# Pre-norm attention and top-2 mixture-of-experts layer on one Trainium2 core: the projected values are copied out of PSUM by ScalarE, and their bias is folded into the output projection's bias

## What is computed

```python
def _L0_attn_ref(x, W_attn, b_attn, W_proj, b_proj):
    qkv = x @ W_attn + b_attn
    q, k, v = jnp.split(qkv, 3, axis=2)
    ...
    q = _rope_as_in_source(q)
    k = _rope_as_in_source(k)
    att = jnp.einsum('bhqd,bhkd->bhqk', q, k) * (1.0 / math.sqrt(hd))
    att = jnp.where(causal[None, None, :, :], att, -jnp.inf)
    att = jax.nn.softmax(att, axis=-1)
    y = jnp.einsum('bhqk,bhkd->bhqd', att, v)
    y = y.transpose(0, 2, 1, 3).reshape(B, T, C)
    return y @ W_proj + b_proj

x = x + _L0_attn_ref(_layernorm(x, axis=-1), ...)
x = x + _L0_ffn_ref(_layernorm(x, axis=-1), ...)
```

## Time and profile before

| | |
|---|---|
| median of 3 runs | 1797.29 us (1796.71 to 1798.85) |
| the profiled execution, its own time | 1802.63 us |
| its span, first to last instruction | 1800.9 us |
| mean granted TensorE clock | 0.976 of full speed |
| instructions | 45470 |
| attention, loop of 16 batches | about 55 to 860 us of the span |

### The profile page before, as it was taken

One profiled execution on the slowest core, in us unless ns is written; L12 is line 12 of the kernel. 1 busy time (PEld: TensorE's weight loads), 2 busy tenths in 40 slices (PEclk: granted clock), 3 DMA queues, 4 the chain that ended last, 5 costly groups with the idle time before them and its releaser, 6 DMA issues.

```text
span 1800.9 us, 45470 instructions
## 1 busy us (share of the span) xinstructions
PE 1636.0 (91%) x15505; PEld 1132.7 (63%) x15507; DVE 1169.6 (65%) x2062; ACT 874.3 (49%) x1273; POOL 780.0 (43%) x1005
## 2 busy tenths in 40 slices
PE   2689999999999999984798999989999999999996
PEld 2345555555555555432575566669999999999985
DVE  5568888888888888874358777874434444443442
ACT  1266666666666666552333222544444444444442
POOL 1023333333333333332200676725666666666652
PEclk9799999999999999987899999999999999999998
DMA  1322333333333333211536553223434333333432
GB/s 58 106 84 83 107 106 107 106 99 101 104 106 107 107 99 96 91 54 43 187 124 185 171 164 88 83 89 54 68 59 66 62 62 66 61 64 61 65 60 25
DMA packets 168709, 163.37 MB, mean 91 GB/s; under 512 B 29682, under 2 KB 159218, under 8 KB 168563
## 3 DMA queue, kind: packets, MB, share of 16 engines
q1 hardware_dynamic: 138354, 125.66, 22.8%
q0 software_dynamic: 30208, 35.81, 12.4%
HBM read 100.82 MB, written 60.30 MB: 89 GB/s over the span
## 4 chain that ended last, share of the span: by engine, by line
PE 68%; DVE 12%; issue 7%; DMA 5%; SPq 4%; ACT 3%; POOL 1%; DVEq 0%; POOLq 0%; ACTq 0%
PE bank L1615 21%; PE pair_s L1980 10%; PE pair_s L1615 7%; PE bank L1980 5%; PE pair_t L1980 5%; PE bank L1749 4%; PE pair_s L1675 3%; SPq L480 2%; PE pair_t L1723 2%; DVE mx L1165 2%; PE pair_t L1969 2%; ACT qkh L861 2%; SPq L472 1%; DMA q_op<-m_row 1%; PE bank L1765 1%
## 5 line engine op out<-in xcount | busy, mean ns | idle before, releaser
L884 ACT ACTIVATE prob<-pair_t 128x1024 f32<-128x1024 f32 x320 | 327.4, 1023 | 243.0 <-PE pair_t L1723 238.3
L702 POOL TENSOR_SCALAR_AFFINE_SELECT prob<-prob 128x256 f32<-128x256 f32 (+1 forms) x448 | 196.8, 453 | 478.0 <-ACT prob L884 466.4
L818 POOL DMA_INDIRECT out_x<-ysb,tok_rows x136 | 218.2, 1605 | 196.2 <-ACT ysb L1025 146.3
L1573 DVE SCALAR_TENSOR_TENSOR early<-pair_s,h_s,sg 128x512 f32<-128x512 f32 (+1 forms) x72 | 51.9, 721 | 249.0 <-PE pair_s L1980 249.0
L780 POOL DMA_INDIRECT tok_d<-tok_w,dest_i x128 | 126.6, 989 | 160.2 <-DVE dest_i L1424 121.5
L1980 PE MATMUL pair_s<-xt,wbuf 128*128 128x256 f16 (+1 forms) x1728 | 193.9, 267 | 1.9 <-DVE xt L1564 1.9
L1615 PE MATMUL bank<-wbuf,early 128*128 x1632 | 190.2, 273 | 0.9 <-ACT ysb L1025 0.8
L1749 PE MATMUL bank<-prob,v_op 128*32 128x512 f32 (+3 forms) x2048 | 181.5, 450 | 2.0 <-POOL prob L702 1.7
L1016 ACT CAST early<-early 128x512 f16<-128x512 f32 (+1 forms) x144 | 85.6, 594 | 196.6 <-DVE early L1573 196.6
L1615 PE MATMUL pair_s<-wsh,xt 128*128 128x512 f16 x768 | 179.2, 382 | 0.0
L1980 PEld LDWEIGHTS pair_s<-xt,wbuf 128*128 x1728 | 163.0, 98 | 22.3 <-issue 2.3
(11 more groups left out here) (259 smaller groups left out, 3090.8 us busy)
## 6 DMA issues: line engine op xcount, KB each, us to landing
q_op<-qk_d SPq DMA_DIRECT2D x192, 64.0 KB, 2.4
k_op<-qk_d SPq DMA_DIRECT2D x192, 64.0 KB, 2.4
x_in<-in_L_attn_x SPq DMA_DIRECT2D x16, 512.0 KB, 4.2
qk_d<-qkh SPq DMA_DIRECT2D x32, 256.0 KB, 2.5
qk_d<-qkl SPq DMA_DIRECT2D x32, 256.0 KB, 2.7
xres<-in_L_attn_x SPq DMA_DIRECT2D x16, 512.0 KB, 4.7
x_d<-x SPq DMA_DIRECT2D x32, 256.0 KB, 2.2
xhl_d<-xhl SPq DMA_DIRECT2D x32, 256.0 KB, 2.5
```

The costliest lines, as they stand in the source:

```text
L702: last = nc.gpsimd.affine_select(out=v, in_=v, compare_op=ALU.is_ge, fill=0.0, base=0, pattern=[[0, v.shape[1]], [1, P]], channel_multipli ...
L818: pool.indirect_dma_start(out=out, out_offset=bass.IndirectOffsetOnAxis(ap=tok_rows[:, k, 0:1], axis=0), in_=ysb[:, k % ROWS_AHEAD], in_of ...
L884: nc.scalar.activation(prob[:, half, u].rearrange("p a n -> p (a n)"), pair_t[:].rearrange("p a n -> p (a n)"), ACT.Exp, scale=exp_by).the ...
```

## The change

ACT's new `values` copies a half of the values in one instruction of 128x512 from PSUM to `v_op`, without a bias; DVE's `values` with its two additions goes. The call keeps its slot in the table, and in ACT's body it stands last among the projection's copies, so behind `normalise` in the same step. The broadcast bias row `bvb` and its DMA go. In the prologue the bias of the values is turned into two more columns of `bcol` by two more one-element matmuls, DVE spreads each column into a 128x128 tile (`bvm`), PE multiplies these with the output weights into `ps_y`, and DVE adds the result to `bpb` once, after the shift of batch 1 and ahead of its loop; POOL's first addition of `bpb` waits for that.

```diff
-        bvb = sb_a("bvb", [P, C], F32)
-        bcol = sb_a("bcol", [P, 4], F32)
+        bcol = sb_a("bcol", [P, 6], F32)
+        bvm = sb_a("bvm", [P, 2, P], F32)
...
-            sp.dma_start(bvb[:], b_attn[2 * C:].unsqueeze(0).broadcast_to([P, C])).then_inc(S["const_in"], 16)
...
-                                        pool.wait_ge(S["const_in"], 48)
+                                        pool.wait_ge(S["bias_done"], 1)
...
+            def values(n, par, j, src=ps_q):
+
+                act.wait_ge(S["v_in"], 2 * n + j + 1)
+                if n == 0:
+                    act.wait_ge(S["v_cleared"], 1)
+                if some(4 * (n - 1)):
+                    act.wait_ge(S["pv_in"], 4 * (n - 1))
+                nc.scalar.copy(v_op[:, par, 2 * j:2 * j + 2, :, 0:HD],
+                               src[:].rearrange("p (t h d) -> p t h d", t=2, d=HD)).then_inc(S["v_done"], 1)
...
-                for i in range(4):
+                for i in range(2):
+                    qk_high(0, i, QK_BANK[i])
+                for j in range(2):
+                    values(0, 0, j, V_BANK[j])
+                for i in range(2, 4):
                     qk_high(0, i, QK_BANK[i])
...
                                 if (g, s) == QK_HIGH[i] and QK_HIGH[i] >= QK[i]:
                                     qk_high(b + 1, i)
+                            for j in range(2):
+                                if (g, s) == VALUES[j]:
+                                    values(b + 1, 1 - par, j)
...
-            def values(n, par, j, src=ps_q):
-
-                dve.wait_ge(S["v_in"], 2 * n + j + 1)
-                if some(4 * (n - 1)):
-                    dve.wait_ge(S["pv_in"], 4 * (n - 1))
-                for t in range(2):
-                    last = nc.vector.tensor_tensor(
-                        v_op[:, par, 2 * j + t, :, 0:HD],
-                        src[:, 256 * t:256 * t + 256].rearrange("p (h d) -> p h d", d=HD),
-                        bvb[:].rearrange("p (h d) -> p h d", d=HD), ALU.add)
-                last.then_inc(S["v_done"], 1)
-
...
-                nc.vector.tensor_copy(bcol[:], ps_m[:, 0:4])
+                link.link(dve, nc.vector.tensor_copy(bcol[:], ps_m[:, 0:6]))
                 link.link(dve, nc.vector.tensor_copy(wah[:], wa[:, 0:2, :]))
                 nc.vector.tensor_tensor(wal[:], wa[:, 0:2, :], wah[:].bitcast(F32),
                                         ALU.subtract).then_inc(S["scales_done"], 1)
+                for c in range(2):
+                    last = nc.vector.tensor_scalar(bvm[:, c, :], ones_f[:], bcol[:, 4 + c:5 + c], None, ALU.mult)
+                last.then_inc(S["bvm_done"], 1)
...
-                dve.wait_ge(S["const_in"], 48)
+                dve.wait_ge(S["const_in"], 32)
...
-                for j in range(2):
-                    values(0, 0, j, V_BANK[j])
...
                 input_shift(1)
+                dve.wait_ge(S["bias_in"], 1)
+                nc.vector.tensor_tensor(bpb[:], bpb[:], ps_y[:, 0:C], ALU.add).then_inc(S["bias_done"], 1)
...
-                            for j in range(2):
-                                if (g, s) == VALUES[j]:
-                                    values(b + 1, 1 - par, j)
...
-                for i in range(4):
-                    col = 256 * (i % 2) + P * (i // 2)
+                for i in range(6):
+                    col = 256 * (i % 2) + P * (i // 2) if i < 4 else 2 * C + P * (i - 4)
...
                     project_qk(0, i, QK_BANK[i])
+                pe.wait_ge(S["bvm_done"], 1)
+                pe.wait_ge(S["const_in"], 32)
+                pe.wait_ge(S["xl_done"], 2)
+                for c in range(2):
+                    last = nc.tensor.matmul(ps_y[:, 0:C], bvm[:, c, :], wp[:, c, :], start=(c == 0), stop=(c == 1))
+                last.then_inc(S["bias_in"], 1)
```

More of the change, by code:

```diff
@@ L247, in build @@
         names = ("k_filled const_in w_in x_in0 x_in1 res_in ops0 ops1 qks0 qks1 "
-                 "pool_const attn_w qk_topped biascols scales_done "
+                 "pool_const attn_w qk_topped biascols scales_done bvm_done bias_in bias_done v_cleared "
                  "xn_done shift_done xnT_in xh_done xl_done qk_in qkh_done qkl_done v_in v_done "
@@ L1097, in prologue @@
                 link.link(dve, nc.vector.memset(mx[:], 0.0))
-                link.link(dve, nc.vector.memset(v_op[:, :, :, :, HD:HD + 1].rearrange(
-                    "p a t h d -> p (a t h) d"), 1.0))
+                nc.vector.memset(v_op[:, :, :, :, HD:HD + 1].rearrange(
+                    "p a t h d -> p (a t h) d"), 1.0).then_inc(S["v_cleared"], 1)
                 stats(0, 0, 0)
```

## The result

| | median | lowest to highest | ratio to the kernel before, 95% interval |
|---|---|---|---|
| kernel before, first comparison | 1797.29 us (5 runs) | 1796.71 to 1799.71 | |
| changed kernel | 1812.33 us (5 runs) | 1812.01 to 2804.05 | 1.007 [1.0057, 1.0083] |
| changed kernel, second comparison | 1811.03 us (before: 1799.98) | 1810.63 to 1813.69 | 1.0064 [1.0047, 1.0081] |
| changed kernel, third comparison | 1813.96 us (before: 1799.93) | 1812.00 to 1817.42 | 1.0081 [1.0061, 1.0100] |

The changed kernel is slower: by 15.0, 11.1 and 14.0 us between medians, and by 12.6, 11.5 and 14.6 us by the ratios, where 14.7 were forecast (1812.0 us).

The account below looks back on a forecast made before the run. PE was taken to bound a batch, busy 47.87 of 50 us. Loop terms 15.5 + 0.1 - 2.6 and prologue +1.7 gave +14.7 us on 1797.3, so 1812.0 us; own range 1807 to 1816, whole range 1804 to 1820.

Parts of the forecast that it names:

- Half 0: Loop step (1,3): ACT's single copy ends sooner than DVE's two additions, gaining 0.17 us a batch, 2.6 us in all.
- The exponential behind it: ACT's exponential after the half 0 copy: ACT is free again at 267.57, before its start at 267.75, so no delay.
- Half 1: Loop step (2,3): copy queues behind two normalisations on ACT, stalling PE 1.11 us in 14 batches, 15.5 us.
- batch 14: Half 1 without normalisations: the copy follows `o_t` directly, ends at 279.86 and costs 0.12 us.
- nothing to absorb it: PE's other waits shift with the stall; rivals: half absorbed, 1804.3 us, chance 0.08; wholly, 1796.5 us, chance 0.05.
- DVE's relief: DVE's freed 0.68 us in (1,3) and 0.69 us in (2,3) were taken to gain zero.
- the rival: Faster by relief of DVE in front of low parts and maxima: 1788.8 us, chance 0.05.
- The prologue: Bias work before the loop: +1.5 us before PE's first projection plus 0.2 us for the `bpb` addition, +1.7 us.
- The wait for the bias columns: Prologue: two more one-element matmuls, four more records of 0.21 us, lengthen DVE's wait by 0.86 us.
- the added wait and the two fills: Prologue, ahead of L1072: 0.11 us for the wait on `bcol`, 0.54 us for two `bvm` fills.
- The addition to `bpb`: Prologue, ahead of the first maximum: between nothing and 0.34 us, taken as 0.2 us.
- the gap on POOL: Prologue, 7.25 us from DVE's variance to POOL's root: moves with the chain; otherwise the estimate is 1.5 us lower.

Follow-up runs that it names:

- the kernel with the copy at (2,2): Changed kernel with ACT's copy of half 1 one step earlier, at (2,2): 1960.62 us against 1962.19, ratio 0.9992; later 1798.85 against 1799.93, ratio 0.9993.
- the two dose experiments: Changed kernel with three or one instead of two normalisations ahead of half 1's copy: 1985.17 us, ratio 1.0120, and 1967.90 us, ratio 1.0032.

## Why the prediction was right

**Half 0, gain of 0.17 us.** Measured 0.17 in the timeline (0.40 against 0.57 us), and 0.17 to 0.27 in the shortest period of the kernel with the copy at (2,2). The exponential behind it was to be late for nothing, and started 0.04 us after PE's shifted scores.

**Half 1, stall of 1.11 us in 14 batches.** Measured 1.12. The sum of both, +0.94 us a batch, came out as +0.96 in the shortest period (+0.90 between the second profiles). In batch 14 the 0.12 us of the forecast measured 0.14. That the wait goes through PE's queue in full, with nothing to absorb it, was argued from the chains behind PE's other waits; the two dose experiments show it, at 0.47 and 0.49 us for a step of 0.50.

**DVE's relief, nothing.** Right, by the kernel in which DVE is kept busy. The rule that the rival leaned on, to use both engines for emptying PSUM (the Trainium skill, TensorEngine Tiling (Array Packing), "PSUM Bottleneck"), is neither borne out nor refuted as a rule: here it gains 0.17 us a batch where ACT is free when the product ends, and loses 1.1 us where it is queued behind other work.

**The prologue, +1.7 us.** The parts hold nearly, but about 1 us of their sum arrives at the loop. DVE and POOL of the changed kernel:

```profile
33.47 0.16 DVE L1138 COPY bcol<-bank 128x6 f32<-128x6 f32 x1 [2.81 <-PE bank L1656]
...
36.34 0.48 DVE L1143 TENSOR_SCALAR bvm<-ones_f,bcol 128x128 f32<-128x128 f32 x2
36.73 1.28 DVE L1088 TENSOR_TENSOR xl<-bank,xh 128x512 fp32r<-128x512 f32 x2
...
51.84 0.17 DVE L1077 TENSOR_SCALAR mv<-mv 128x4 f32<-128x4 f32 x1
...
60.69 0.42 DVE L1159 TENSOR_TENSOR bpb<-bpb,bank 128x256 f32<-128x256 f32 x1
61.02 1.22 DVE L1172 TENSOR_REDUCE mx<-pair_s 128x2 f32<-128x1024 f32 x1
```

```profile
13.03 0.28 POOL L642 TENSOR_SCALAR_AFFINE_SELECT ident<-ident 128x128 f32<-128x128 f32 x1 [11.36 <-issue]
...
59.52 1.05 POOL L675 TENSOR_TENSOR rstd<-mv,neghalf 128x4 f32<-128x4 f32 x1 [31.18 <-issue]
```

The wait for the bias columns is 2.81 us instead of 1.96, +0.85 (0.86 forecast). From `bcol` to L1088 it is 3.26 us instead of 2.74, +0.52 (0.65 forecast for the added wait and the two fills; the fills take 0.39 of it, start to start). The addition to `bpb` holds the first maximum up by 0.33 (0.2 forecast). That is +1.7. Yet the first maximum is at 61.02 and was at 61.35. First, the whole chain hangs on POOL's first select, and that one starts at 13.0 to 14.4 us from trace to trace; in the trace of before:

```profile
14.22 0.28 POOL L643 TENSOR_SCALAR_AFFINE_SELECT ident<-ident 128x128 f32<-128x128 f32 x1 [12.54 <-issue]
```

Counted from there, L1088 comes 1.4 us later with the bias work in every trace: 23.69 to 23.73 us in ten, against 22.32 and 22.35 in the two of the kernel before and 22.32 with the work off the path. The maximum comes after 47.99 us instead of 47.13 (second profiles: 48.86 and 47.81), so only +0.9 and +1.05 of the +1.7 are left there; over the ten traces it is 47.63 to 49.01. The rest goes in two places that vary from trace to trace. One is the gap on POOL, below. The other is the way from L1088 to the end of the variance, 15.28 us instead of 16.40 (16.20 and 16.38 in the second profiles), in which PE's first products run: their records go from 0.63 to 0.39 us each, and this happens at 41.7 us in the changed kernel's trace and at about 44 us before, while the granted clock reads 1.00 in both. Over the traces, the sooner it happens after L1088 the shorter that way is; in both traces of the kernel before it happens latest. Why is not shown.

**The gap on POOL moves with the chain.** From the variance's end to the root it is 7.25 us before and 7.51 after, 7.91 and 7.44 in the second profiles, and over the 13 traces used here it is 7.15 to 7.91 us while the variance ends anywhere from 51.56 to 53.94. So it isn't a time of its own that would swallow a delay. The Trainium skill (GPSIMD Engine Reference, "Instruction dispatch") gives about 6 us for the first call of a freshly loaded routine, without an instruction of its own in the profile. A gap of that kind is what the traces have, somewhat longer; that a load fills it no run shows.

**The total.** 14 times 0.96, and about 1 us from the prologue, is 14.4 us; measured 15.0, 11.1 and 14.0 between medians. The ratios' intervals are 10.2 to 14.9, 8.5 to 14.6 and 11.0 to 18.0 us: the first and the third hold the forecast difference of 14.7, the second just ends below it. That the forecast is on the high side fits two readings above: the prologue gives 1 us instead of 1.7, and averaged over all twelve periods the batch grows by 0.75 to 0.98 us instead of 1.11 less 0.17. Whether a tenth of a us of each stall is given back in the longer batches isn't settled.

## What to carry to other kernels

If the engine that bounds the stage waits for a piece of work, moving that work from a nearly full engine to one with free time pays only as far as it is done sooner, not by the load that it shifts: read the timeline of the taking engine around the slot, and find at what place in its in-order queue the moved instruction will stand. Price the move as the end of the last instruction ahead of it, plus its own duration, minus the time at which its reader wants it. A call in a step's body can be as good as free one line higher, or one step earlier: here the same copies cost about 10 us more behind two normalisations than in front of them.

## What the runs showed of the hardware that wasn't expected

- The first select on POOL starts 11.4 to 12.7 us after the instruction before it, differently in each launch, and the prologue follows it one to one: the copy of the bias columns starts 20.43 to 20.46 us after it in ten traces with the bias work, in which the select itself lies between 13.03 and 14.35. A change of 1 us in that prologue can't be read from one trace without counting from there.
- Two fills of 128x128 fp32 with a scalar by column took 0.39 us from the first one's start to that of the next instruction, so 0.20 us each, below the 0.27 that was taken.
- A one-element fp32 product costs PE 0.42 us here (two records, 0.21 us apart): six take 0.85 us more than four.
